# A linear-attention state kept as 16 tiles of 32x32 in 128x128, and its products made on the array's diagonal

## The reference

```python
def step(kv, inp):                       # kv: 32 x 32 per head, over blocks of tokens
    qi, ki, vi = inp
    qkv_none_diag = (qi * q_decay) @ kv                  # what the state gives
    qk = (qi @ ki.T) * diag_decay
    qkv_diag = qk @ vi                                   # what the block gives
    kv_new = block_decay * kv + (ki * k_decay).T @ vi
    return kv_new, qkv_none_diag + qkv_diag
```

## Time and profile before

| | |
|---|---|
| median of 3 runs | 521.44 us (521.37 to 521.46) |
| the profiled execution's own time | 522.22 us |
| its span in the profile | 520.5 us |
| PE, DVE, ACT, POOL busy | 490.6, 304.1, 230.3, 216.2 us |
| slots of chunks 0 to 15 | 54.6 to 312 us, about 16.8 us each up to chunk 13 |

### The profile page before, as it was taken

The page is one execution under the profiler, slowest core; times in us unless marked ns, Lnnn a source line. Parts: engine busy times, 40 slices in busy tenths (PEclk is TensorE's granted clock), DMA queues, the critical chain, the costliest instruction groups (busy, mean ns, idle before and its releaser), DMA issues.

```text
span 520.5 us, 10501 instructions
## 1 busy us (share of the span) xinstructions
PE 490.6 (94%) x4143; PEld 448.1 (86%) x4143; DVE 304.1 (58%) x615; ACT 230.3 (44%) x404; POOL 216.2 (42%) x191
## 2 busy tenths in 40 slices
PE   6986999999999999999998988999999989999984
PEld 6976999899998998989988877898888778999773
DVE  5958468664479888662646565987675426230231
ACT  7820241212245766512232426465758765453330
POOL 3012235323023311325066666644426332778882
PEclk9997999999999999999999997999999999999999
DMA  7914242133300110002412543565556622455423
GB/s 253 372 44 128 74 122 70 55 103 102 122 23 21 45 42 21 21 21 83 161 42 83 184 161 137 169 212 172 203 173 219 215 82 82 141 163 162 161 82 40
DMA packets 32880, 62.05 MB, mean 119 GB/s; under 512 B 3440, under 2 KB 3456, under 8 KB 32704
## 3 DMA queue, kind: packets, MB, share of 16 engines
q1 hardware_dynamic: 32288, 60.08, 35.0%
q0 software_dynamic: 544, 1.31, 1.4%
HBM read 48.27 MB, written 13.12 MB: 118 GB/s over the span
## 4 chain that ended last, share of the span: by engine, by line
PE 74%; POOL 5%; issue 4%; ACT 3%; DVE 3%; DMA 3%; DVEq 0%; ACTq 0%; POOLq 0%
PE bank L1211 24%; PE bank L1165 8%; PE bank L1202 8%; PE bank L1167 8%; PE bank L1166 7%; POOL wlo L1103 4%; PE bank L1230 3%; PE bank L1274 3%; PE bank L1264 3%; PE bank L1258 3%; ACT whi L514 2%; PE bank L1421 1%; PE bank L1251 1%; DMA raw<-in_w_gate 1%; PE bank L1181 1%
## 5 line engine op out<-in xcount | busy, mean ns | idle before, releaser
L1103 POOL TENSOR_TENSOR wlo<-raw,whi 128x512 fp32r<-128x512 f32 x96 | 127.9, 1364 | 92.0 <-ACT whi L514 92.0
L1088 POOL TENSOR_TENSOR state<-kv_new,state_dec 128x512 f32<-128x512 f32 x15 | 21.8, 1452 | 126.6 <-DVE kv_new L790 126.6
L1165 PE MATMUL bank<-HTh,whi 128*128 128x256 f32 x224 | 66.2, 296 | 1.9 <-ACT whi L514 1.2
L1167 PE MATMUL bank<-HTh,wlo 128*128 128x256 f32 x224 | 64.3, 287 | 0.0
L1166 PE MATMUL bank<-HTl,whi 128*128 128x256 f32 x224 | 64.3, 287 | 0.0
L779 DVE TENSOR_TENSOR A<-bank,DEC 128x512 f32<-128x512 f32 x64 | 39.7, 682 | 31.0 <-PE bank L1230 29.9
L514 ACT ACTIVATE whi<-raw 128x2048 fp32r<-128x2048 f32 x24 | 45.8, 1910 | 22.9 <-DMA raw<-in_w_down 14.4
L1165 PEld LDWEIGHTS bank<-HTh,whi 128*128 128x128 f32 x224 | 44.0, 197 | 3.3 <-issue 2.7
L1211 PE MATMUL bank<-xTh,WKh 128*128 128x256 f32 x128 | 38.7, 302 | 6.5 <-DVE xTl L712 6.5
L1166 PEld LDWEIGHTS bank<-HTl,whi 128*128 128x128 f32 x224 | 44.0, 196 | 0.3
L1167 PEld LDWEIGHTS bank<-HTh,wlo 128*128 128x128 f32 x224 | 43.9, 196 | 0.0
(11 more groups left out here) (237 smaller groups left out, 1344.4 us busy)
## 6 DMA issues: line engine op xcount, KB each, us to landing
X<-in_x SPq DMA_DIRECT2D x16, 256.0 KB, 4.2
xn_all<-XN SPq DMA_DIRECT2D x16, 256.0 KB, 2.8
uo_all<-uo SPq DMA_DIRECT2D x16, 256.0 KB, 2.6
raw<-in_wq SPq DMA_DIRECT2D x4, 1024.0 KB, 5.3
UR<-uo_all SPq DMA_DIRECT2D x16, 256.0 KB, 4.6
XR<-in_x SPq DMA_DIRECT2D x16, 256.0 KB, 2.9
out<-XR SPq DMA_DIRECT2D x16, 256.0 KB, 2.0
raw<-in_wo SPq DMA_DIRECT2D x4, 1024.0 KB, 5.8
```

The lines of the kernel that those rows point to most:

```text
L1088: Q.tensor_tensor(state[:], kv_new[:], state_dec[:], ALU.add).then_inc(state_ok, 1)
L1103: ins = Q.tensor_tensor(low[:, k, :], raw[b % 2][:, k, :], high[:, k, :].bitcast(f32), ALU.subtract)
L1165: T.matmul(dst, lh, rh, start=first, stop=False)
L1167: return T.matmul(dst, ll, rh, start=False, stop=last)
```

## The change

`state` and `state_dec` shrink from four tiles of 128x128 to 128 partitions by 4x32: row 32r+i of group j holds head 4j+r, and nothing off the diagonal is stored. Three things follow.

In `attend`, the state's part is 16 matmuls, one per head, each on the 32x32 tile of the array at row group r and column group r, with 32 of the contraction and 128 columns. All write the same bank, each group r its own 32 partitions.

In `new_keys_values`, 16 matmuls with a contraction of 128 write 32x32 each, on column tiles 128x32, with 32 moving columns. The result fills 128 of the bank's 512 columns.

The mask, its setup on POOL (one memset, two selects) and its semaphore are gone. The sum of the new part and the decayed state is done by DVE, from the bank, where the mask multiplication stood; POOL keeps the decay alone, at 128x128. Keys turned now wait for the state and not for the mask.

```diff
--- before.py
+++ after.py
@@ -99,11 +99,11 @@
 
         DEC, A = (at(n, kb, [P, NH, P]) for n, kb in (("DEC", 158), ("A", 166)))
         QD, KD = at("QD", 174, [P, NK, P]), at("KD", 176, [P, DM])
-        qdec, sq, state, state_dec, kv_new = (at(n, kb, [P, NK, P]) for n, kb in (
-            ("qdec", 178), ("sq", 180), ("state", 184), ("state_dec", 186), ("kv_new", 188)))
+        qdec, sq = (at(n, kb, [P, NK, P]) for n, kb in (("qdec", 178), ("sq", 180)))
+        state, state_dec = (at(n, kb, [P, NK, DH]) for n, kb in (("state", 184), ("state_dec", 186)))
         kdec = at("kdec", 182, [P, DM])
         uo = at("uo", 190, [P, 2, NK, P])
-        BM, sq_sum = at("BM", 194, [P, P]), at("sq_sum", 194.5, [P, P])
+        sq_sum = at("sq_sum", 194.5, [P, P])
         SM, PR, PN = (at(n, kb, [P, 2, 3 * P]) for n, kb in (("SM", 166), ("PR", 169), ("PN", 172)))
         PT = at("PT", 175, [P, 2, 3 * P])
         OTh, OTl = (at(n, kb, [P, 2, SEL], f32r) for n, kb in (("OTh", 181), ("OTl", 183)))
@@ -259,7 +259,7 @@
         picked, scattered = sems("picked scattered")
 
         consts, iota_ok, masks_ok, tok_ok, lag_ok = sems("consts iota_ok masks_ok tok_ok lag_ok")
-        decays_ok, dec_ok, bm_ok, causal_ok = sems("decays_ok dec_ok bm_ok causal_ok")
+        decays_ok, dec_ok, causal_ok = sems("decays_ok dec_ok causal_ok")
 
         k_w_hi, k_w_lo, q_w_hi, q_w_lo, v_w_hi, v_w_lo = sems("k_w_hi k_w_lo q_w_hi q_w_lo v_w_hi v_w_lo")
         u_w_hi, u_w_lo, o_w_hi, o_w_lo = sems("u_w_hi u_w_lo o_w_hi o_w_lo")
@@ -268,7 +268,7 @@
         xt_ps, xt_hi, xt_lo, proj_ps, proj_sb = sems("xt_ps xt_hi xt_lo proj_ps proj_sb")
 
         q_dec, kt_ps, k_dec = sems("q_dec kt_ps k_dec")
-        s_ps, masked, inter_ps, kv_ps, kv_masked, pv_ps = sems("s_ps masked inter_ps kv_ps kv_masked pv_ps")
+        s_ps, masked, inter_ps, kv_ps, pv_ps = sems("s_ps masked inter_ps kv_ps pv_ps")
         state_dk, state_ok, uo_ok, sq_ok, sum_sq, rms_ps, ms_ok, r_ok = sems(
             "state_dk state_ok uo_ok sq_ok sum_sq rms_ps ms_ok r_ok")
         uo_hi, uo_lo, out_ps, base_ok, final_ok = sems("uo_hi uo_lo out_ps base_ok final_ok")
@@ -276,7 +276,7 @@
         turned_ps, turned_ok, compared, tied, counted = sems("turned_ps turned_ok compared tied counted")
         rank_ok, cnt_ps, oh_ok, idx_ps, idx_ok, pick_read = sems("rank_ok cnt_ps oh_ok idx_ps idx_ok pick_read")
 
-        dve_chain, pool_chain = sems("dve_chain pool_chain")
+        dve_chain, pool_chain, state_zero = sems("dve_chain pool_chain state_zero")
 
         fw_hi, fw_lo = sems("fw_hi fw_lo")
         var_s_ok, r_s_ok, hs_ok, ht_ps, tab_ps = sems("var_s_ok r_s_ok hs_ok ht_ps tab_ps")
@@ -784,11 +784,11 @@
                 dve.wait_ge(kt_ps, N + 1), dve.wait_ge(kv_ps, N)
                 V.tensor_tensor(kdec[:], turn_bank[:], KD[:], ALU.mult).then_inc(k_dec, 1)
 
-            def state_part(N):
-
-                dve.wait_ge(kv_ps, N + 1), dve.wait_ge(state_ok, N)
-                V.tensor_tensor(kv_new[:], tiles4(turn_bank[:]), BM[:].unsqueeze(1).to_broadcast([P, NK, P]), ALU.mult)\
-                    .then_inc(kv_masked, 1)
+            def new_state(N):
+
+                dve.wait_ge(kv_ps, N + 1), dve.wait_ge(state_dk, N + 1)
+                V.tensor_tensor(state[:], turn_bank[:, 0:P].rearrange("p (k e) -> p k e", k=NK), state_dec[:], ALU.add)\
+                    .then_inc(state_ok, 1)
 
             def gated(N):
 
@@ -909,7 +909,6 @@
                 router(M)
             dve.wait_ge(decays_ok, 4), dve.wait_ge(masks_ok, 2)
             V.tensor_tensor(DEC[:], DEC[:], tri[:].unsqueeze(1).to_broadcast([P, NH, P]), ALU.mult).then_inc(dec_ok, 1)
-            dve.wait_ge(bm_ok, 1)
             for N in slots_of_chunks:
                 if N >= 0:
                     mask(N)
@@ -948,7 +947,7 @@
                 if N >= 0:
                     gated(N)
                 if 0 <= N < N_TILES - 1:
-                    state_part(N)
+                    new_state(N)
                 if N >= N_TILES - CH:
                     in_position(N, 2)
                 if N == HIDDEN + 1:
@@ -1078,14 +1077,9 @@
 
             def state_decayed(N):
 
-                pool.wait_ge(state_ok, N), pool.wait_ge(bm_ok, 1), pool.wait_ge(decays_ok, 3)
-                Q.tensor_tensor(state_dec[:], state[:], bdec.unsqueeze(2).to_broadcast([P, NK, P]), ALU.mult)\
+                pool.wait_ge(state_ok, N), pool.wait_ge(state_zero, 1), pool.wait_ge(decays_ok, 3)
+                Q.tensor_tensor(state_dec[:], state[:], bdec.unsqueeze(2).to_broadcast([P, NK, DH]), ALU.mult)\
                     .then_inc(state_dk, 1)
-
-            def new_state(N):
-
-                pool.wait_ge(kv_masked, N + 1), pool.wait_ge(state_dk, N + 1)
-                Q.tensor_tensor(state[:], kv_new[:], state_dec[:], ALU.add).then_inc(state_ok, 1)
 
             def gather():
 
@@ -1104,15 +1098,7 @@
                 ins.then_inc(fw_lo, 1)
 
             ln_rstd(range(CH))
-            Q.memset(state[:], 0.0)
-            Q.memset(BM[:], 1.0).then_inc(pool_chain, 1)
-            blocks = BM[:].rearrange("p (r m) -> p r m", r=4)
-            pool.wait_ge(pool_chain, 5)
-            Q.affine_select(out=blocks, in_=blocks, compare_op=ALU.is_ge, fill=0.0, base=0, pattern=[[-DH, 4], [0, DH]],
-                            channel_multiplier=1).then_inc(pool_chain, 1)
-            pool.wait_ge(pool_chain, 6)
-            Q.affine_select(out=blocks, in_=blocks, compare_op=ALU.is_ge, fill=0.0, base=DH - 1,
-                            pattern=[[DH, 4], [0, DH]], channel_multiplier=-1).then_inc(bm_ok, 1)
+            Q.memset(state[:], 0.0).then_inc(state_zero, 1)
             ln_rstd(range(CH, NXN))
             for N in slots_of_chunks:
                 if ln_tiles(N):
@@ -1125,8 +1111,6 @@
                     gather()
                 if N >= N_TILES - 3:
                     block_lo(2 * (N - (N_TILES - 3)))
-                if 0 <= N < N_TILES - 1:
-                    new_state(N)
                 if -1 <= N < N_TILES - 1:
                     state_decayed(N + 1)
                 if N >= N_TILES - 3:
@@ -1246,16 +1230,18 @@
 
             def keys_turned(N):
 
-                pe.wait_ge(xt_lo, min(N + XT_AHEAD, N_TILES)), pe.wait_ge(kv_masked, N)
+                pe.wait_ge(xt_lo, min(N + XT_AHEAD, N_TILES)), pe.wait_ge(state_ok, N)
                 for k in range(NK):
                     ins = T.transpose(turn_bank[:, k * P:(k + 1) * P], chunk(KT, N)[:, k, :], ident[:])
                 ins.then_inc(kt_ps, 1)
 
             def attend(N):
 
-                pe.wait_ge(q_dec, N + 1), pe.wait_ge(state_ok, N), pe.wait_ge(bm_ok, 1), pe.wait_ge(ms_ok, N)
-                for j in range(NK):
-                    ins = T.matmul(out_bank[:, j * P:(j + 1) * P], state[:, j, :], qdec[:, j, :], start=j == 0,
+                pe.wait_ge(q_dec, N + 1), pe.wait_ge(state_ok, N), pe.wait_ge(state_zero, 1), pe.wait_ge(ms_ok, N)
+                for h in range(NH):
+                    j, r = h // 4, h % 4
+                    rows = slice(DH * r, DH * r + DH)
+                    ins = T.matmul(out_bank[rows, j * P:(j + 1) * P], state[rows, j, :], qdec[rows, j, :], start=j == 0,
                                    stop=False, skip_group_check=True)
                 ins.then_inc(inter_ps, 1)
                 pe.wait_ge(proj_sb, NPROJ * (N // CH) + 6), pe.wait_ge(masked, 4 * N + 4)
@@ -1269,10 +1255,11 @@
             def new_keys_values(N):
 
                 pe.wait_ge(k_dec, N + 1), pe.wait_ge(xt_lo, min(N + XT_AHEAD + 1, N_TILES))
-                for j in range(NK):
-                    cols = slice(j * P, (j + 1) * P)
-                    ins = T.matmul(turn_bank[:, cols], kdec[:, cols], VT[N // CH % 2][:, N % CH, cols], start=True,
-                                   stop=True)
+                for h in range(NH):
+                    j, r = h // 4, h % 4
+                    cols = slice(DH * h, DH * h + DH)
+                    ins = T.matmul(turn_bank[DH * r:DH * r + DH, j * DH:(j + 1) * DH], kdec[:, cols],
+                                   VT[N // CH % 2][:, N % CH, cols], start=True, stop=True)
                 ins.then_inc(kv_ps, 1)
 
             def scores_turned():
```

## The result

The changed kernel takes 509.47 us (median of 4 runs, 508.66 to 510.31) where the kernel before took 521.45 in the same series. The ratio on record is 0.9753 (95% interval 0.9724 to 0.9781; the two medians alone divide to 0.9770, inside it). On the 521.44 us stated above the ratio gives 508.6 (507.1 to 510.0). A second series of the same kernel gave 0.9733 (0.9704 to 0.9761). The profiled execution took 509.0 us with a span of 507.3, 13.2 less than before.

A forecast was written before the change was run, and what follows sets the result against it. PE's own stream was taken to bound 14 slots, with PE waiting only in the last. Gains of 7.6 + 2.6 - 0.1 = 10.1 us off the profiled 522.22 gave 512.1, median 511.3; own range 509.5 to 513.5, wider one 509.0 to 520.3.

The forecast's parts named there:

- One slot: PE's state, values and new keys: 3.23 us becomes 2.69, a gain of 0.54 in each of 14 slots.
- 7 x 0.03 + 0.02 = 0.23: New keys on PE: 32 records in 8 passes of four tiles take 0.23 us a slot.
- The pass of 0.03: New keys on PE: a pass of four tiles takes 0.03 us, between bounds of 0.028 and 0.11.
- The diagonal's 0.81: State's part on PE: 32 diagonal records, four side by side, take 0.81 us, as the values do.
- the changes of form: PE's switches of tile form: 0.21 us into 32x32, then 0.20 from 32x32 to 128x32.
- the 0.09 ahead of the keys: PE between values and new keys: both are column tiles, so no change of form, only 0.09 us.
- B: Rival: diagonal tiles can't write one bank at once; 3.41 us instead of 0.81 a slot, 552.9 us in all; chance 0.10.
- C: Rival: a matmul's two records stay together, only two tiles overlap in state and new keys; 528.7 us; chance 0.05.
- A: Rival: small matmuls don't get cheaper; 0.025 us a record, new keys 0.78 instead of 0.23; 519.0 us; chance 0.07.
- The last slots: Slots 14 and 15: less POOL and DVE work shortens PE's waits, 2.6 us up to unit 5.
- slot 15's 0.1: Slot 15 has no new keys and only pays the diagonal's extra 0.1 us.
- nothing is edited ... I let all of it move along: Behind slot 15: first wait hangs on chunk 15's values, so all moves along, with no gain of its own.

The follow-up runs named there:

- keys_only: The kernel before, with the new keys alone in tiles of 32 columns; state, mask and POOL's work at full width: 512.6 us, ratio 0.981.
- diag_only: The kernel before, with the state's product alone on 32x32 diagonal tiles; new keys, mask and POOL as before: 524.38 us, ratio 1.0035.
- late_pool: The changed kernel with two unused GpSimd operations of 128x512 ahead of the decay in chunks 13 and 14: 514.32 us, ratio 0.9835.
- pool_only: The kernel before, with the addition of the state moved from POOL to DVE at full width: 521.54 us, ratio 0.9988.
- phase_before: The kernel before with 208 unneeded PE instructions more in the gap of chunk 0: 520.23 us, ratio 0.9937.
- phase_after: The changed kernel with 48 unneeded PE instructions more in the gap of chunk 0: 512.21 us, ratio 0.9787.

## Why the prediction was right, and where it was wrong

- **One slot.** Forecast 0.54 us, measured 0.49 in the stretch of chunk 9. The term that was mis-sized is the new keys' "7 x 0.03 + 0.02 = 0.23", which measured 0.283: 0.05 a slot, or 0.65 of the 0.8 us by which the 13 slots fell short. The pass of 0.03 itself was right. In every slot of both profiles the starts of the first seven passes lie 0.031 us apart (0.187 for six steps), and it is the last pass and a bit, from 0.187 to 0.283, that is slower; why, no run shows. The diagonal's 0.81, the changes of form (0.21 and 0.20 forecast, 0.209 and 0.198 measured) and the 0.09 ahead of the keys held. That all the gain is in the new keys, and that the state's part costs 0.1, is shown by keys_only and diag_only.
- **The bank.** The diagonal tiles share one bank at full rate. B, for which I kept 0.10, and C are out; so is the reading of the Trainium skill's "TensorEngine Tiling (Array Packing)", "Gotcha 1: PSUM Pressure", under which this case would have been B: 32 records, four row groups, one bank, 0.81 us from first start to last.
- **The 25 ns.** A is out: starts in four tiles lie 0.009 us apart on average (0.283 over 31). The Trainium skill, "TensorE: Matmul & The Clock Gate", section "Wait — 56ns, not 53.3ns?", gives a floor of about 25 ns from start to start; by these rows it can hold for one tile at most.
- **The last slots.** Forecast 3.1 us for slots 13 and 14 together, slot 15's 0.1 taken off, measured 2.8, with the waits where they were named. late_pool makes GpSimd's work ahead of the blocks the cause of about 2, in part by an estimate. pool_only shows that its order alone isn't enough: with the operations at full width 0.3 is gained.
- **Behind slot 15.** This is the step that failed: "nothing is edited ... I let all of it move along". It moved along for 128 us and then gained 2.9, a term that the sum put at nothing. The reason is one that no row of mine showed: the change adds 1488 PE instructions, and with them the later instruction fetches come elsewhere among the transfers of weights. Blocks 17, 20 and 23 took 6.2 to 6.4 us with a fetch early in them and take 5.0 to 5.2 with one at their end. phase_before gets this gain without the change, and phase_after takes it from the change. In ratios it is 0.9733 with that gain and 0.9787 without; the latter is 510.3 on the 521.44 us of before, 1.0 under the forecast.
- **The start.** 1.1 us in the profile, of which DVE's shorter normalization can be 0.6; it isn't resolved in times.

So of the 13.2 us between the two profiles 9.0 are in the slots and are the change's own mechanism, where 10.1 were forecast; 2.9 are luck of alignment that the kernel before could have had too; and of the other 1.3 the start has 1.1, mostly unresolved. The forecast median was off by less than the terms were, since a shortfall of 1.1 in the slots hid part of the 2.9.

## What to carry to other kernels

Price small matmuls by the changes of tile form around them as well as by their columns: here four 32-wide tiles ran side by side even into one bank, and a change of form between neighbours cost 0.2 us, so groups of one form belong next to each other. When a stretch that nobody edited moves by a per cent, count instructions: look in the DMA view for the instruction queue beside the transfer that is late. And before a structure is judged by under 1%, run it with some tens of idle instructions more, to see how much of the difference is alignment.

## What the runs showed of the hardware that was not expected

- Instruction fetches of 16 KB, 0.9 to 1.7 us each, hold up data transfers. A transfer of 1 MB with one early in it ends 0.9 to 1.5 us later (4.9 to 5.4 becomes 6.1 to 6.5) in all eight cases of the table; in its six cases from 4.37 us on the fetch does nothing.
- PE adds one such fetch for 256 instructions. An fp32 matmul is four instructions (12 of them added 48 to the page's count) and a bf16 one two (104 added 208).
- A DVE operation of 128x512 with one operand takes 1.25 us beside a GpSimd operation of that size and 0.61 beside one of a quarter. The Trainium skill, "Advanced Engine Details and Errata", section "DVE Details", says that one of DVE's two ports is shared with GpSimd; the trace agrees so far as these rows go.
- After a wait of PE of 2.4 to 3.1 us ahead of unit 5 the granted clock was half of 2.4 GHz for 3.4 to 6.8 us in four profiles of five; after the changed kernel's wait of 1.43 us there it stayed full. Behind the next long wait, 2.4 us in all thirteen, it fell in six and stayed in seven, so the length of the wait alone doesn't decide it.
